# Causal mask: from four small TensorE products per tile to VectorE's own pass over the scores

## The reference

```
q, k, v = x @ Wq, x @ Wk, x @ Wv          # 16 query heads, 4 key/value heads, D = 128
scores = rotary(q) @ rotary(k).T * D**-0.5
scores = where(causal, scores, most negative float)
y      = softmax(scores) @ v
o      = 0.5*y + 0.5*o_gla                 # o_gla: a gated linear attention over the same q, k, v
out    = concat(o) @ Wo
```

## Time and profile before

| | |
|---|---|
| median of 3 runs | 973.99 us (973.38 to 974.23) |
| the profiled execution, its own time | 972.46 us |
| its span | 970.6 us |
| TensorE busy | 925.6 us (95%) |
| VectorE busy | 653.2 us (67%) |
| ScalarE busy | 661.7 us (68%) |
| GpSimd busy | 634.5 us (65%) |
| TensorE granted clock, mean | 0.985 |

### The profile page before, as it was taken

One profiled execution on the slowest core, in us unless ns is written; L12 is line 12 of the kernel. 1 busy time (PEld: TensorE's weight loads), 2 busy tenths in 40 slices (PEclk: granted clock), 3 DMA queues, 4 the chain that ended last, 5 costly groups with the idle time before them and its releaser, 6 DMA issues.

```text
span 970.6 us, 18411 instructions
## 1 busy us (share of the span) xinstructions
PE 925.6 (95%) x5347; PEld 717.4 (74%) x5347; DVE 653.2 (67%) x1598; ACT 661.7 (68%) x2138; POOL 634.5 (65%) x609
## 2 busy tenths in 40 slices
PE   7899999999999999999999999999999988998991
PEld 4677778787878787878878777777778766776770
DVE  4776767676767676767676969676978774452284
ACT  6677777777777777777777767786768674454452
POOL 6868685767565657676767768775658883536452
PEclk9899999999999999999999999999999999999996
DMA  7101100000000000900000000010102111233363
GB/s 252 34 17 34 39 1 1 7 12 6 1 0 0 0 0 6 252 18 1 1 2 1 1 6 8 1 63 1 63 2 74 50 59 55 82 89 118 111 197 114
DMA packets 34066, 43.20 MB, mean 45 GB/s; under 512 B 3772, under 2 KB 27966, under 8 KB 33856
## 3 DMA queue, kind: packets, MB, share of 16 engines
q1 hardware_dynamic: 30240, 33.76, 12.0%
q0 software_dynamic: 3744, 8.43, 2.5%
HBM read 25.58 MB, written 18.43 MB: 45 GB/s over the span
## 4 chain that ended last, share of the span: by engine, by line
PE 86%; ACT 4%; DVE 4%; issue 3%; DMA 2%; POOL 1%; another core or an unknown queue 0%; POOLq 0%; SPq 0%; DVEq 0%; ACTq 0%
PE OA L597 13%; PE PR L480 12%; PE S L550 11%; PE MS L570 10%; PE S L579 7%; PE S L696 5%; PE OA L559 5%; PE OA L713 4%; PE OA L590 4%; PE PR L526 3%; PE PR L520 3%; PE S L541 1%; PE MS L509 1%; DMA acc<-in_x_rows 1%; ACT eqk L828 1%
## 5 line engine op out<-in xcount | busy, mean ns | idle before, releaser
L1500 POOL TENSOR_TENSOR qd<-eqk,eg 128x512 f32<-128x512 f32 x63 | 74.9, 1189 | 161.8 <-issue 155.4
L597 PE MATMUL OA<-wT,V 128*128 128x512 f32 x320 | 149.2, 597 | 0.0
L790 ACT ACTIVATE S<-S,nm 128x128 f32<-128x128 f32 (+3 forms) x256 | 126.9, 496 | 28.7 <-DVE nm L1003 25.4
L828 ACT ACTIVATE eqk<-qkv,nmx 128x128 f32<-128x128 f32 x320 | 124.4, 396 | 3.4 <-DVE nmx L1078 2.9
L1003 DVE TENSOR_REDUCE nm<-S 128x2 f32<-128x256 f32 (+3 forms) x128 | 102.0, 817 | 30.7 <-PE S L550 24.7
L1488 POOL TENSOR_TENSOR eqk<-eqk,rse 128x640 f32<-128x640 f32 x63 | 79.6, 1264 | 52.8 <-DVE rse L1121 31.5
L597 PEld LDWEIGHTS OA<-wT,V 128*128 128x128 f32 x320 | 59.7, 191 | 69.4 <-issue 68.9
L1037 DVE TENSOR_TENSOR pr<-S,rl 128x256 f32<-128x256 f32 (+3 forms) x128 | 105.5, 824 | 5.0
L1477 POOL TENSOR_TENSOR rp<-qkv,cos 128x640 f32<-128x640 f32 x64 | 99.6, 1556 | 6.6 <-ACT qkv L818 4.9
L1480 POOL TENSOR_TENSOR rp<-rp,rt 128x640 f32<-128x640 f32 x64 | 99.6, 1556 | 5.0
L1477 POOL TENSOR_TENSOR rt<-qkv,sin 128x640 f32<-128x640 f32 x64 | 99.3, 1552 | 0.0
(11 more groups left out here) (174 smaller groups left out, 2499.4 us busy)
## 6 DMA issues: line engine op xcount, KB each, us to landing
qkv<-slot_x SPq DMA_DIRECT2D x46, 129.0 KB
pr<-plane SPq DMA_DIRECT2D x16, 256.0 KB, 2.8
gu_w<-in_wgu SPq DMA_DIRECT2D x8, 352.0 KB, 3.4
slot_x<-zero SPq DMA_DIRECT2D x2, 1290.0 KB, 9.4
stage<-in_wqkv SPq DMA_DIRECT2D x6, 384.0 KB, 3.5
xraw<-in_x_cols SPq DMA_DIRECT2D x16, 128.0 KB, 2.4
acc<-in_x_rows SPq DMA_DIRECT2D x1, 2048.0 KB, 11.5
dn_w<-in_wdn SPq DMA_DIRECT2D x8, 256.0 KB, 4.2
```

The lines of the kernel that those rows point to most:

```text
L597: last = pe.matmul(OA[:, :], V[:, j, :], wT[:, j, :], start=(c == 0 and j == 0), stop=(j == c))
L790: nc.scalar.activation(S[:, h, 0:n], S[:, h, 0:n], ACT.Exp, bias=nm[:, h:h + 1], scale=1.0, accum_out=ls[:, h:h + 1]).then_inc(s_exp, 1)
L828: last = nc.scalar.activation(eqk[:, par, h * 128:(h + 1) * 128], qkv[:, c % C, h * 128:(h + 1) * 128], ACT.Exp, bias=nmx[:, h:h + 1], sca ...
```

## The change

`maskb` becomes one row of 512 columns: 384 zero columns and the 128x128 triangle. TensorE's L541 goes, the first score product of a head now starts the bank, and s_sc counts heads (four per step), not pairs. VectorE's `score_max` runs once per head: one custom instruction adds the mask to the head's scores, negates, writes the result back in place and takes the minimum, which is the negated maximum; then a second instruction reads the accumulator out into `nm`. ScalarE's exponential waits per head and uses scale -1. VectorE's groups 1 to 6 are written out, not looped.

```diff
-        maskb = sb("maskb", [P128, 2, P128], BF16)
+        maskb = sb("maskb", [P128, N], BF16)
...
-                for h in range(GQ):
-                    pe.matmul(S[:, h, n - 128:n], maskb[:, 0, :], maskb[:, 1, :], start=True, stop=False, skip_group_check=True)
...
-                        last = pe.matmul(S[:, h, 0:n], q[:, h * 128:(h + 1) * 128], k[:, 0:n], start=False,
-                                         stop=(i == len(steps) - 1), skip_group_check=True)
-                    if h % 2:
-                        last.then_inc(s_sc, 1)
+                        last = pe.matmul(S[:, h, 0:n], q[:, h * 128:(h + 1) * 128], k[:, 0:n], start=(i == 0),
+                                         stop=(i == len(steps) - 1))
+                    last.then_inc(s_sc, 1)
...
-                    if h % 2 == 0:
-                        act.wait_ge(s_nm, 2 * u + 1 + h // 2)
-                    nc.scalar.activation(S[:, h, 0:n], S[:, h, 0:n], ACT.Exp, bias=nm[:, h:h + 1], scale=1.0,
+                    act.wait_ge(s_nm, 4 * u + 1 + h)
+                    nc.scalar.activation(S[:, h, 0:n], S[:, h, 0:n], ACT.Exp, bias=nm[:, h:h + 1], scale=-1.0,
...
-            def score_max(g, c, pair):
+            def score_max(g, c, h):
                 u = C * g + c
                 n = P128 * (c + 1)
-                dve.wait_ge(s_sc, 2 * u + 1 + pair)
+                dve.wait_ge(s_sc, 4 * u + 1 + h)
                 later(dve, s_exp, 4 * u)
-                nc.vector.tensor_reduce(nm[:, 2 * pair:2 * pair + 2], S[:, 2 * pair:2 * pair + 2, 0:n], AX_X, ALU.max,
-                                        negate=True).then_inc(s_nm, 1)
+                nc.vector.tensor_tensor_reduce(out=S[:, h, 0:n], in0=S[:, h, 0:n], in1=maskb[:, N - n:N], scale=-1.0,
+                                               scalar=FAR, op0=ALU.add, op1=ALU.min, accum_out=nm[:, h:h + 1]).then_inc(s_nm, 1)
...
                 score_max(g, c, 0)
+                score_max(g, c, 1)
                 if c == 0 and not first:
                     o_low(g - 1, C - 1)
-                score_max(g, c, 1)
+                score_max(g, c, 2)
+                score_max(g, c, 3)
...
-            with dve.Fori(1, PEEL) as g:
+            for g in range(1, PEEL):
                 for c in range(C):
                     step(g, c)
```

More of the change, by code:

```diff
@@ L66 @@
 NEG = -1.0e30
+FAR = 3.0e38
 YO = 5
@@ L382, in _ @@
             sp.dma_start(cm[:, :], cmat).then_inc(s_cst, 16)
-            sp.dma_start(maskb[:, :, :], cmask).then_inc(s_cst, 16)
+            sp.dma_start(maskb[:, :], cmask).then_inc(s_cst, 16)
             sp.dma_start(wTf, wo_in[:, 0:2048]).then_inc(s_wor, 16)
@@ L854, in q_out @@
                 act.wait_ge(s_trq, u + 1)
-                later(act, s_sc, 2 * u)
+                later(act, s_sc, 4 * u)
                 nc.scalar.copy(rq_hi[:, :] if c % C else rqT[:, :], PR[:, 0:512]).then_inc(s_rqT, 1)
@@ L1097, in k_out @@
                 dve.wait_ge(s_trk, u + 1)
-                later(dve, s_sc, 2 * u)
+                later(dve, s_sc, 4 * u)
                 later(dve, s_at, u)
@@ L1668 @@
     bf16 = mybir.dt.np(BF16)
-    cmask = np.stack([(s == t).astype(f32), np.where(t > s, f32(NEG), f32(0.0))], axis=1).astype(bf16)
+    cmask = np.concatenate([np.zeros((P128, N - P128), f32), np.where(t > s, f32(NEG), f32(0.0))], axis=1).astype(bf16)
     named = {"x_rows": x, "x_cols": x.T, "wqkv": wqkv.reshape(P128, KV, KT2 * QKV), "wo_in": wo.reshape(P128, H * HID),
```

## The result

The changed kernel takes 969.19 us (median; 968.50 to 969.81), the kernel before 973.99: a ratio of 0.9957, 95% interval 0.9942 to 0.9971, or 4.8 us less by the medians. Its profiled execution has an own time of 969.53 us and a span of 967.7, 2.9 less than before. The granted clock of TensorE is 0.985 in both.

What follows compares the result with a forecast made beforehand. TensorE was taken to bound c = 0, TensorE and others alike c = 1 and 2, VectorE's chain to gc c = 3. Terms -3.1 - 0.1 + 5.9 - 3.5 - 0.5 = -1.3 us gave 972.7 us, range 965.5 to 983.

Steps and rivals of the forecast that it cites:

- c = 0: First step of a group, bound by TensorE alone: the removed mask products gain 0.22 us in 14 steps, -3.1 us.
- X: VectorE's extra time per step for four fused instructions and reads in place of two maxima: 0.14 + 4e, 0.42 us.
- c = 2: Step where VectorE's chain to gc is as long as TensorE's: X lost in 14 steps, +5.9 us.
- c = 3: Step bound by VectorE's chain to gc: waits per head bring gc 0.23 us earlier in 15 steps, -3.5 us.
- The forecast's own band: Whole kernel with e between 0.045 and 0.10: 969.5 to 976.5 us, chance 0.42.
- e: VectorE's time for the accumulator read behind each fused instruction: taken as 0.07 us, between 0.01 and 0.17.
- the rival with a nearly free accumulator read: VectorE's read costs only e = 0.01 to 0.045, so the kernel takes 965.5 to 969.5 us; chance 0.24.
- c = 1: Step where pr and qd come just in time: small TensorE gains, X lost in three late steps, sum -0.1 us.
- the last step: Final step: behind the last scores VectorE handles one head (0.68 us) instead of a 1024-element maximum (1.14), -0.5 us.
- The unrolled loop: VectorE's groups 1 to 6 written out: 0, at most 0.6 us either way.
- the wider mask: One load of 128 KB beside the start-up loads: 0 us.
- the rival with 1.5 ns an element: The fused instruction runs slower per element than a plain maximum, about +25 us in all; chance 0.04.

Runs made afterwards that it cites:

- e5_after_again: The changed kernel itself, unchanged, run again on another chip: 962.89 us against 968.31 for the kernel before, ratio 0.9954.
- e1: Kernel before with only VectorE's groups 1 to 6 written out instead of looped: 967.97 us against 967.49, ratio 1.0003.
- e3: Kernel before with the mask products left out at c = 1 alone, those scores not masked: 967.03 us, ratio 0.9997.
- e11: Changed kernel with a small extra VectorE instruction behind each of the four fused ones at c = 0 alone: ratio 1.0047 to the kernel before.

## Why the prediction was right, and where its terms were off

The mechanism was right: TensorE gains the products at c = 0, loses VectorE's X at c = 2, and gains by the finer waits at c = 3. The direction was that of the centre, but the size was not: -1.3 was forecast, less than could be told from no change, and -4.8 was measured. The forecast's own band (969.5 to 976.5, chance 0.42) did not hold. The time, 969.19, and the measured e both lie in the band of the rival with a nearly free accumulator read (965.5 to 969.5, chance 0.24), so which side of no change it would fall on was left to one unmeasured term. Its own ledger, in us:

| | forecast | the same formula with e = 0.035 | measured, u = 4 to 63 |
|---|---|---|---|
| c = 0 | -3.1 | -3.1 | -4.1 |
| c = 1 | -0.1 | -0.5 | +1.0 |
| c = 2 | +5.9 | +3.9 | +3.9 |
| c = 3 and the last step | -4.0 | -6.0 | -4.4 |
| sum | -1.3 | -5.7 | -3.5 |

(The measured column ends at the last step's L567 and so leaves out what comes behind it there.) With e put right the formula goes too far: c = 1 and c = 3 gave 3.1 us less than it says, c = 0 gave 1.0 more. That its errors pull against each other is luck.

**e, the accumulator's read: 0.07 forecast, 0.035 measured.** This is the mis-sized term. Three of the four fused instructions of a step stand behind a read and pay 0.04, am behind the last one 0.01 to 0.02. X is 0.29 (2.02 - 1.73), not 0.42. In the typical step the formula is then borne out: at c = 2 typically +0.29, at c = 3 -0.51 + 4 x 0.035 = -0.37, and -0.37 was measured. ScalarE's read, the row that I weighed against the memsets, holds its queue for 0.09; VectorE's runs beside its successor. The Trainium skill's Vector Engine (DVE) Microarchitecture Reference, Measured stream behaviour on trn2, gives about 75 ns for each instruction; from that figure X would be an estimated 0.14 + 4 x 0.075 = 0.44. The trace agrees with that page for the fused instruction itself (a distance of 0.47 at n = 384, 0.40 of it for the elements), and not for the read behind it.

**c = 0: the price was read too small.** 0.22 is the distance from L541 to L550; the matmuls overlap at their ends, and what TensorE gained, measured from the gather, is 0.27, in 14 of the 15 steps (0.22 in step 56).

**c = 1: the step that failed.** I had TensorE gain until it met pr or qd, and 0.22 in full where L616 covers pr. It gained nothing, since it already waited for rq_lo ahead of the scores, and the mask products lay inside that wait; the run without them at c = 1 shows it. The typical +0.05, in the groups 1 to 6, is no loss of time: the kernel before with its loop unrolled has it too, in the same steps, and is no slower for it; L601 starts that much earlier and waits for rq_lo that much longer. In the three late steps with routing work there was a loss as said, but smaller than the 0.42 each: +0.26, +0.15 and +0.39. Of the last a part is TensorE's clock: the granted clock was 0.50, its lower level (1.2 GHz), from 777.4 on, where step 61 began, and in e5_after_again, with the clock at 1.00 there, it is +0.18.

**c = 3: not every step had room.** In steps 7 and 47 L567 came 0.06 and 0.04 later, not 0.37 earlier. There the chain to gc was full from the start: Ut began 1.7 us behind the first score product in place of 1.3, so VectorE no longer waited for scores and paid X. The forecast had 15 steps with room. In step 47 routing work stood ahead (L1184 to L1189, up to 0.92 us behind the start of L598). In step 7 what came late was gl, VectorE's features of the gates, held by GpSimd:

```profile
107.90 1.82 POOL L1526 TENSOR_TENSOR w_lo<-stage,w_hi 128x768 fp32r<-128x768 f32 x1
...
108.56 1.31 DVE L1124 SCALAR_TENSOR_TENSOR gl<-qkv,lnp 128x128 f32<-128x128 f32 x1 [0.69 <-ACT lnp L837]
109.79 0.68 DVE L991 TENSOR_TENSOR oT_lo<-OA,oT_hi 128x512 fp32r<-128x512 f32 x1
```

**The last step**, against the earlier trace rows, in the kernel after:

```profile
809.52 0.73 DVE L999 CUSTOM_DVE_ANT_0 S<-S,maskb 128x512 f32<-128x512 f32 x1
...
810.16 0.69 DVE L1006 TENSOR_TENSOR am<-OA,cm 128x512 f32<-128x512 f32 x1
```

From the last maximum to am are 0.64 us in place of 1.14, the -0.5 of the forecast. On the path it was worth less. In the first trace of the kernel before the second maximum of this step began 4.49 us behind L601, in e1 and e3, where this step is the same, at 3.46; why, no run shows. It was not a slower pace of TensorE, as the forecast had it: the score products start 0.23 apart there as in other steps c = 3, with a granted clock of 1.00. Against e3 the changed kernel (e5) starts L576 0.36 earlier, 7.64 for 8.00.

**The rest.** The unrolled loop and the wider mask: 0, shown for the loop; the mask's load was not tried by itself. The fused instruction's rate is that of the plain one, which ends the rival with 1.5 ns an element. By groups, the fused instructions and their reads are 154.6 us where the maxima were 102.0; VectorE's busy time, in which overlaps count once, rose by 13.5 us, not by the 30 to 50 forecast.

**What stays open.** The traces differ by 2.9 us and the medians by 4.8; the interval of the ratio, 2.8 to 5.6 us, holds both, and the profiled execution of the kernel before was itself 1.5 below its median. The last steps differ between executions. From L567 of step 60 to that of step 63 are 37.4 us in the first trace of the kernel after and 36.6 in e5, and for the kernel before 34.7 in the first trace and 36.2 in e3, which differs from it at c = 1 alone. In the kernel after the granted clock was 0.50 from 777.4 on and again from 797.9 on; in the kernel before it was 1.00 at both places and 0.50 from 814.8 on. So at step 60 the changed kernel is 3.4 us ahead, at step 63 0.7, at the start of the expert work 3.1. And of the 7.6 us of the early gc in the kernel before, 5.3 are placed, the rest are not.

## What to carry to other kernels

Price work that is taken off the busiest engine at each place where it stands: here the same four products were worth 0.27, 0, 0 and 0.3 us at four steps of one loop, and what decided was who was waited for next. If the work moves to an engine whose chain is just in time there, first clear that chain (two reordered lines at no cost): the same change then brought 8.6 us in place of 4 to 5. To tell whether a chain is just in time, give it a dose and see whether its reader moves, but look at what the dose itself waits for.

## What the runs showed of the hardware that was not expected

VectorE's read of its accumulator shares its start with the next instruction: it has 142 ns of busy time, but costs 0.04 us in front of another fused instruction and 0.01 to 0.02 in front of am.

A VectorE instruction with two sources in SBUF did not end before the GpSimd TENSOR_TENSOR that was running when it started: a dose took 0.17 us alone and 0.96 beside eqk (it ended 0.04 us behind it), gl 0.27 alone and 1.31 beside w_lo (0.15 behind it). The fused instruction, with one source in PSUM and one in SBUF, is not held: at c = 0 of the kernel after it took 0.30 us from 221.66, 0.01 behind the start of GpSimd's 1.26 us, and its usual time in all 70 cases of that trace where such an instruction of GpSimd had more than 0.3 us to go. This fits the Trainium skill, SBUF — State Buffer, SBUF: two separate sides, which has the two engines share a pair of ports; whichever starts first holds it for its whole instruction, and VectorE with two SBUF inputs contends there with a GpSimd instruction that reads SBUF. In one point the traces differ from that page: beside GpSimd's TENSOR_SCALAR on acc (L1559) in e11 a dose took 0.18 us with 0.57 of that instruction to go, so not each GpSimd instruction holds VectorE. By that page the choice of PSUM and SBUF for the fused instruction's sources, which I had weighed only for its rate, is also what keeps it clear of GpSimd.
